# Causal attention: the row maxima of a group of heads in reverse query order

## What is computed

```python
attn = jnp.einsum('bhqd,bhkd->bhqk', q, k) * scale      # 16 heads of 16
attn = jnp.where(causal, attn, -jnp.inf)                # keys up to the query
# _custom_softmax:
a = jnp.clip(a, -100.0, 100.0)
m = jnp.max(a, axis=-1, keepdims=True)
e = jnp.exp(a - m)
p = e / (jnp.sum(e, axis=-1, keepdims=True) + 1e-06)
p = p + 1e-08
p = p / jnp.sum(p, axis=-1, keepdims=True)
```

## Time and profile before

| | us |
|---|---|
| median of three runs | 2610.97 (2608.83 to 2614.83) |
| the profiled execution's own time | 2617.94 |
| its span, first to last instruction | 2616.2 |
| TensorE busy | 2440.0 (93%) |
| VectorE busy | 1836.5 (70%) |
| ScalarE busy | 1439.2 (55%) |
| GpSimd busy | 1350.9 (52%) |

### The profile page before, as it was taken

How to read it: one execution, slowest core, us unless ns; L and a number is a source line. 1 busy time by engine, 2 the same in 40 slices (tenths; PEclk the granted TensorE clock), 3 DMA queues, 4 the chain that set the end, 5 groups by cost and what they waited for, 6 DMA issues and landing times. The chain is left out here.

```text
span 2616.2 us, 46472 instructions
## 1 busy us (share of the span) xinstructions
PE 2440.0 (93%) x15044; PEld 1418.3 (54%) x15044; DVE 1836.5 (70%) x3685; ACT 1439.2 (55%) x2991; POOL 1350.9 (52%) x1358
## 2 busy tenths in 40 slices
PE   6999999999999999989899699987999999989998
PEld 3555555554444444349799366653344444358897
DVE  4989998999778888844343558867778888844333
ACT  3666666666777777653233223214777777653332
POOL 5356665563234545445555569843334445435555
PEclk8999999999999999999999789988999999999999
DMA  5333333333434444234555200015434444245554
GB/s 159 100 100 108 105 102 105 111 99 101 118 110 132 130 128 124 84 114 166 199 181 174 70 1 17 17 54 138 119 110 128 129 129 125 72 134 168 182 196 139
DMA packets 249938, 305.91 MB, mean 117 GB/s; under 512 B 28034, under 2 KB 224865, under 8 KB 249700
## 3 DMA queue, kind: packets, MB, share of 16 engines
q1 hardware_dynamic: 238164, 275.37, 35.2%
q0 software_dynamic: 10176, 26.27, 2.8%
q10 hardware_dynamic: 1360, 1.31, 0.2%
HBM read 210.32 MB, written 92.84 MB: 116 GB/s over the span
## 5 line engine op out<-in xcount | busy, mean ns | idle before, releaser
L769 DVE TENSOR_REDUCE neg_max_af<-sc_af 128x1 f32<-128x512 f32 (+3 forms) x864 | 551.8, 665 | 111.7 <-PE sc_af L474 85.1
L690 ACT ACTIVATE prob_af<-sct_af 128x512 f32<-128x512 f32 (+1 forms) x864 | 484.9, 582 | 250.5 <-PE sct_af L495 138.1
L769 DVE TENSOR_REDUCE neg_max_f<-sc_f 128x1 f32<-128x512 f32 x512 | 334.2, 685 | 92.4 <-PE sc_f L474 89.6
L690 ACT ACTIVATE prob_f<-sct_f 128x512 f32<-128x512 f32 x512 | 291.3, 598 | 137.0 <-PE sct_f L495 134.8
L474 PE MATMUL sc_af<-stack_k_af,stack_q_af 96*128 96x512 bf16 (+3 forms) x1024 | 331.9, 344 | 18.4 <-DVE neg_max_af L769 13.6
L495 PE MATMUL sct_af<-stack_q_af,stack_k_af 99*128 99x512 bf16 (+3 forms) x1024 | 331.5, 346 | 6.3 <-ACT prob_af L690 4.9
L1599 PE MATMUL y_ps_e<-w_r,hT_e 128*128 x1120 | 258.6, 384 | 8.8 <-issue 5.0
L798 DVE SCALAR_TENSOR_TENSOR prob_af<-prob_af,w_r 128x512 f32<-128x512 f32 (+2 forms) x224 | 231.9, 1043 | 25.9 <-ACT prob_af L690 25.7
L526 PE MATMUL out_af<-prob_af,v_aug_af 128*32 128x512 f32 (+3 forms) x2048 | 232.3, 525 | 6.8 <-DVE prob_af L798 5.9
L1599 PEld LDWEIGHTS y_ps_e<-w_r,hT_e 128*128 128x128 f32 x1120 | 209.6, 192 | 39.8 <-issue 13.3
L495 PEld LDWEIGHTS sct_af<-stack_q_af,stack_k_af 99*128 99x128 bf16 x1024 | 100.1, 98 | 229.8 <-ACT prob_af L690 147.7
(11 more groups left out here) (382 smaller groups left out, 4732.3 us busy)
## 6 DMA issues: line engine op xcount, KB each, us to landing
w_r<-in_f_W_dram SPq DMA_DIRECT2D x66, 1024.0 KB, 6.4
stack_k_af<-k_parts_d SPq DMA_DIRECT2D x64, 384.0 KB, 4.2
k_parts_d<-parts_af SPq DMA_DIRECT2D x187, 128.0 KB
q_parts_d<-parts_af SPq DMA_DIRECT2D x96, 128.0 KB
stack_q_af<-q_parts_d SPq DMA_DIRECT2D x64, 192.0 KB, 3.0
stack_k_f<-k_parts_d SPq DMA_DIRECT2D x32, 384.0 KB, 4.3
w_next<-in_f_W_dram SPq DMA_DIRECT2D x12, 1024.0 KB
k_parts_d<-parts_f SPq DMA_DIRECT2D x91, 128.0 KB
```

Of the source, the lines that this page charges most:

```text
L690: nc.scalar.activation(dst, src.rearrange("p (h q) -> p h q", h=len(heads)), ACT.Exp).then_inc(S.exp_done, 1)
L769: nc.vector.tensor_reduce(M.neg_max[:, qt, heads[0]:heads[-1] + 1], src, AX.X, ALU.max, negate=True).then_inc(S.max_done, 1)
```

## The change

In a causal batch the slot with key block kt takes the maxima of query block 3 - kt. The same 11 units of `score` and `row_max` are computed, in the order four of 512 keys, four of 384, two of two heads by 256, one of four heads by 128. The opening does the same for its two groups. `max_unit` numbers the units in the new order, the wait for the loaded `stack` rows moves to the new first unit, and `split_max` waits for the new last one. Batches that are not causal keep their order.

```diff
+    def queries_at(n, kt):
+
+        return KT - 1 - kt if causal(n) else kt
@@ max_unit
-        at = (0, 1 + i // 2, 3 + i, 7 + i)[qt] if causal(n) else 4 * qt + i
+        at = (10, 8 + i // 2, 4 + i, i)[qt] if causal(n) else 4 * qt + i
@@ score
-                if qt == 0 and i == 0:
+                if qt == queries_at(n, 0) and i == 0:
                     pe.wait_ge(S.stack_loaded[g], 64 * (n + 1))
@@ TensorE slot
-                        score(tn, tg, kt, i)
+                        score(tn, tg, queries_at(tn, kt), i)
@@ TensorE opening, groups 0 and 1
-                    score(first, 0, qt, i)
+                    score(first, 0, queries_at(first, qt), i)
@@ split_max
-                dve.wait_ge(S.max_done, max_unit(n, g, 3, 3) + 1)
+                dve.wait_ge(S.max_done, max_unit(n, g, queries_at(n, KT - 1), 3) + 1)
@@ VectorE slot
-                        row_max(tn, tg, kt, i)
+                        row_max(tn, tg, queries_at(tn, kt), i)
@@ VectorE opening
-                        row_max(first, g, qt, i)
+                        row_max(first, g, queries_at(first, qt), i)
```

More of the change, by code:

```diff
@@ L570, in _ @@
                 for i in range(4):
-                    score(first, 1, qt, i)
+                    score(first, 1, queries_at(first, qt), i)
                 if qt < 3:
```

## The result

The changed kernel takes 2623.51 us (median of 9 runs, 2616.05 to 2630.26) against 2611.53 (9 runs, 2604.45 to 2614.83): ratio 1.0047 [1.0032, 1.0063], 12 us slower. The forecast was 8 us slower, 2619. The execution of after that was profiled took 2623.51 us.

What follows compares the result with a forecast made beforehand. TensorE was taken as the bound, with VectorE never idle in slots 15 to 3. Terms 7.0 - 0.9 + 1.0 + 2.0 + 1.2 - 0.4 gave about +10, taken as +8: 2611 becomes 2619 us, range 2606 to 2631.

Steps and rivals of the forecast that it cites:

- the crossing: Slots 15 to 3 between batches: later clip and longer chain enlarge TensorE's waits by 1.0 us, seven times, +7.0.
- The chain: VectorE's small chain, moved into slot 15 under GpSimd's splits, takes 2.9 us instead of 2.1, priced by the opening's 3.1.
- The strict lockout: Rival, 12%: each step of slot 15's chain waits for a whole GpSimd split; chain 4.3 us, kernel 2629 us.
- One hole in slot 3 and none for a bank: Expected sign: one hole of about 2 us before slot 3's `pv`, none for a `sc` bank.
- TensorE, sum 0: Slots kt = 0 to 3 change by +0.67, +0.22, -0.22 and -0.67 us, summing to 0 over a group.
- Slot 5, -0.9 in all: In batches 3 and 4 slot 5's 0.45 us hole goes, as VectorE enters slot 4 with the chain done.
- Slot 8, +0.15: TensorE reaches slot 8's transposes 0.17 us earlier while ScalarE's normalised x does not move; seven times +0.15, +1.0.
- Slots 11 to 13, +0.3: Slot 11's chain falls under GpSimd's addition of v, and slot 12 has a residual addition; 0.3 in seven batches, +2.
- the announced sign of error: Prediction counts as wrong if holes appear in slots kt = 1 or 2 of quiet groups, priced at nothing.
- Dips, all seven: Clock dips behind slot 3 in all seven batches, two more than before; 0 to +2.4 us, taken as +1.2.
- Opening, -0.4: VectorE's tail of reductions before the opening's first small chain shortens; 0 to -2 us, taken as -0.4.
- The predicted batch of 71.5 to 72.5: Expected sign: a batch of about 71.5 to 72.5 us, with dips behind slot 3 in all seven.

Runs made afterwards that it cites:

- A1: Changed kernel with GpSimd's three split instructions cut from 512 to 8 columns in causal batches after the first; 2591.51 us.
- B1: Kernel before the change with the same cut of GpSimd's splits from 512 to 8 columns; 2591.87 us.
- C1: Kernel before with only group 1 reversed (maxima made in slots 12 to 15 and in the opening); -0.05% against before.
- C2: Kernel before with only group 2 reversed (maxima made in slots 0 to 3); +0.43% against before.
- A2: Changed kernel, GpSimd waiting for slot 15's small chain before its split and slot 11's before the sum of v; 0.57% less time than the changed kernel.
- E1: Changed kernel with only split j = 3, which runs in slots 4 and 5, cut to 8 columns; batch 0.7 us shorter, time no faster.
- D3: Changed kernel with both GpSimd holds and slot 12's residual addition moved ahead of the first reduction; 0.9964 [0.9945, 0.9983] of before.
- A3: Changed kernel with only GpSimd's split held behind slot 15's chain, and slot 12's residual addition ahead of the first reduction; batch 70.87 us.

## Why the prediction came out as it did, step by step

The sign and the place were right, and of the mechanism the first part: VectorE is the bound where GpSimd runs its splits, the moved chain is held there, and without full splits (A1, B1) nothing is lost. The way by which the delay reaches TensorE was wrong (the crossing, below). The size was 8 for 12 us. By the terms:

- *The chain.* Put at 2.9 us between bounds of 1.0 and 3.1; it measured 3.65, outside them. The opening's 3.1 was no upper end: in its chain two steps were held by a split (0.97 and 1.01) and one by a shorter addition (0.65), here three by splits (1.13, 1.02, 1.02). The strict lockout had it at 4.3: in length the truth lies midway, in mechanism it is the strict case. The chain runs behind three splits in turn and ends 6.1 us into slot 15 (348.40 - 342.26), where the strict rival had 6.4 and the forecast 5.0; it begins at 2.5, where both had 2.1. The page on the shared port pair in the Trainium skill ("SBUF — State Buffer") was the better guide than my nearest row, and the trace agrees with it: reductions kept their 0.6 us, small steps waited for whole instructions.
- *The crossing, +1.0.* This is the step that failed. The added-up work came out: from clip to clip it is 363.49 - 343.62 = 19.9 us, where 18.8 + 0.8 = 19.6 was predicted. That is partly luck. The sum does not set slot 3's clip: in C1 it ends as far into slot 3 as before with 2 us less of reductions and 1.5 us more of chain, and C2, whose chain is 2.1, has the changed kernel's hole, 1.75. So no run shows the chain's +0.8 reaching slot 3. Slot 3's hole grew from 1.0 to 1.75, of which TensorE's earlier asking is about 0.5 (1.4 us into the slot, where it was 1.9) and the later clip 0.2. And I held the work against one deadline, slot 3's. VectorE must also have finished the clip of slot 1 by slot 1's `pv`, and the reversed group puts four of 512 and more ahead of it. So group 2 grew by 1.69, not 1.0, with 0.92 us of hole in slot 1. The reversed group shows it without the moved chain in C2 (slot 1: 6.07), the moved chain without the reversed group shows no hole in C1; both with the change in the amount of work named there. In A2, with four reductions in slot 0 and a chain of 1.0, neither slot 0 nor slot 1 has a hole, so the four reductions alone do not make these two holes: the locked chain is needed as well, or the splits where the hold doesn't move them. "One hole in slot 3 and none for a bank" was wrong, and holes in slots kt = 0 and 1 are what the strict rival had foretold.
- *TensorE, sum 0.* It was -0.87 us a batch (-0.3 in slots 0 to 3 and in 12 to 15, less in the others). Slot kt = 0 of group 2 grew by 0.54 and not 0.67, kt = 2 shrank by 0.32 and not 0.22, kt = 3 by 0.75 and not 0.67 (A1 against B1); why, stays open. To slot 8 of batch 7 TensorE's busy time is 8.9 us less, 2.2 of them before batch 1; without that the loss would have been larger by about as much.
- *Slot 5, -0.9 in all.* Wrong in sign: its hole grew from 0.38 to 0.67. VectorE enters slot 4 with the chain done, but later, and with four reductions of 512 ahead of the clips there too; E1 shows that the split beside it is needed for the hole.
- *Slot 8, +0.15:* +0.18 in the hole (0.53 to 0.71). *Slots 11 to 13, +0.3:* 0.66 in slot 13; the cause named (chain under GpSimd's addition, and the residual addition) is confirmed by D3, which removes both, and each alone was not enough. This was also the announced sign of error, a hole in a slot kt = 1 of a quiet group.
- *Dips, all seven.* Four of seven, before five; their number did not follow the holes, their price did (1.6 against 1.18), so the +1.2 was +0.6. *Opening, -0.4:* -1.0, and -0.9 in batch 0.

The predicted batch of 71.5 to 72.5 against 72.53 without a dip came out near by errors that partly cancel.

## What to carry to other kernels

Hold the work of a saturated engine against every deadline on the way, not only the last: a reordering that conserves the sum can still put more ahead of an early one. A chain of short dependent steps belongs where the engine that it is held up by (here GpSimd) is idle, and if it can't move, let that engine wait for its end: here a hold of 1.6 us on GpSimd went with 1.66 us off the batch (A2; A3, with only this one of the two holds, has the same 70.87). On the kernel before the same holds gained nothing that is clear of noise. Two sub-changes that each alter the amount of work in a stretch don't separate its causes, even if their ratios add up. Before reading a fraction of a per cent as an order's merit, take out what the clock did.

## What the runs showed that I had not expected

VectorE and GpSimd hold each other for whole instructions: a chain step of 0.18 us that began inside one of GpSimd's instructions lasted up to 1.24 us and ended within 0.1 us of that instruction's end; a step that began in the gap between two of them kept its 0.18 us. Five such steps took 1.0, 2.1, 2.5 (slot 11 of the changed kernel) and 3.65 us by place alone. Beside VectorE's clips GpSimd pays as well: its 1.67 at 344.18 is an instruction that takes 1.15 where VectorE leaves it alone.

The clock's dips are not a function of the hole's length. Holes of 1.75 us in slot 3 had one behind them in four of seven batches, 0.5 + 0.5 us in five of seven, and a kernel with 1.03 (A3) had none where another with the same slots (A2) had two. Between the length of a batch with one and without one lay 1.0 us (D3) to 3.5 (C2). In E1's batch 4 the granted clock read 0.50 from 362 to 366 us, the lower of its two levels, 1.2 in place of 2.4 GHz, behind the 1.75 us hole.
